# An attention mask added by VectorE in PSUM instead of by a matmul, with two steps of the tile loop moved forward, in a one-core audio tower kernel

## The reference

```python
h = tok_ref(x, W, b)                       # path signature of depth 4, projected to 128
h = h + attn_ref(layernorm(h), ...)        # 8 heads of 64, inner 512
h = h + ffn_ref(layernorm(h), ...)         # 8 experts, top 1, and a shared expert

# in attn_ref, for each sequence
dots = einsum('bhid,bhjd->bhij', q, k) * exp(temperature)
dots = where(eye(n), NEG_MAX, dots)        # a step does not see itself
attn = softmax(dots, axis=-1)
out = einsum('bhij,bhjd->bhid', attn, v)

# in tok_ref, the signature levels of the steps (k = 0..3)
acc = levels[k] + e[k]
for i in range(k): acc = acc + outer(levels[i], e[k - 1 - i])
```

## Time and profile before

| | |
|---|---|
| median of 3 runs | 694.17 us (692.53 to 695.29) |
| the profiled execution | 691.94 us |
| its span in the trace | 690.1 us |
| mean granted TensorE clock | 0.985 |
| first pass of the loop on TensorE | starts at 44.31 us |
| last pass (tile 31) | starts at 488.62 us |
| instructions | 13988 |

### The profile page before, as it was taken

How to read it: one execution, slowest core, us unless ns; L and a number is a source line. 1 busy time by engine, 2 the same in 40 slices (tenths; PEclk the granted TensorE clock), 3 DMA queues, 4 the chain that set the end, 5 groups by cost and what they waited for, 6 DMA issues and landing times.

```text
span 690.1 us, 13988 instructions
## 1 busy us (share of the span) xinstructions
PE 647.0 (94%) x3964; PEld 519.6 (75%) x3997; DVE 420.6 (61%) x1110; ACT 295.9 (43%) x702; POOL 322.1 (47%) x336
## 2 busy tenths in 40 slices
PE   5999999999999999999999999999789989999993
PEld 4677887788878888788877887776578957777772
DVE  7876666666666666766656666766436235455451
ACT  4234455434544445444454344443646334434340
POOL 2455454544545445444545444448534014545453
PEclk9999999999999999999999999999999999999997
DMA  8611344333634334343343431112354113232230
GB/s 308 270 35 31 78 104 95 90 93 76 146 83 99 84 80 118 77 107 76 93 105 83 100 77 39 34 36 73 99 195 138 43 46 44 37 44 39 39 40 5
DMA packets 70133, 59.70 MB, mean 87 GB/s; under 512 B 6752, under 2 KB 58848, under 8 KB 69728
## 3 DMA queue, kind: packets, MB, share of 16 engines
q1 hardware_dynamic: 63472, 55.21, 30.2%
q0 software_dynamic: 6640, 4.22, 4.4%
HBM read 16.78 MB, written 26.30 MB: 62 GB/s over the span
## 4 chain that ended last, share of the span: by engine, by line
PE 83%; DVE 6%; issue 4%; POOL 4%; DMA 1%; ACT 0%; SPq 0%; ACTq 0%; DVEq 0%; POOLq 0%
PE bank L1217 74%; PE bank L1539 3%; PE bank L1273 2%; PE bank L1426 2%; POOL sorted_rows L485 1%; POOL z L470 1%; PE bank L1522 1%; PE bank L1332 1%; PE bank L1323 0%; PE bank L1278 0%; POOL z L472 0%; PE bank L1277 0%; POOL out L558 0%; DVE utl L777 0%; DVE z L883 0%
## 5 line engine op out<-in xcount | busy, mean ns | idle before, releaser
L1217 PE MATMUL bank<-whigh,uth 128*128 128x512 f32 x512 | 169.1, 411 | 1.2 <-DVE lowt L777 1.2
L1217 PEld LDWEIGHTS bank<-whigh,uth 128*128 128x128 f32 x512 | 92.4, 190 | 28.0 <-issue 7.4
L558 POOL DMA_INDIRECT out<-prob,ids x39 | 60.9, 1561 | 94.0 <-ACT prob L740 92.5
L1217 PE MATMUL bank<-whigh,utl 128*128 128x512 f32 x256 | 101.6, 397 | 0.0
L479 POOL TENSOR_TENSOR rstd<-rstd,powers 128x1 f32<-128x1 f32 x64 | 35.3, 552 | 119.8 <-DVE rstd L870 64.5
L470 POOL TENSOR_TENSOR z<-z 128x512 f32<-128x512 f32 x32 | 42.3, 1323 | 90.9 <-DVE z L883 90.9
L1217 PE MATMUL bank<-xT,qkw 128*128 128x128 f32 x512 | 63.9, 279 | 0.0
L1190 DVE COPY xvp<-bank 128x512 f32<-128x512 f32 x39 | 27.0, 692 | 59.3 <-PE bank L1539 59.3
L1217 PEld LDWEIGHTS bank<-xT,qkw 128*128 128x128 f32 x512 | 61.3, 196 | 0.1
L1217 PEld LDWEIGHTS bank<-whigh,utl 128*128 128x128 f32 x256 | 48.4, 189 | 11.9
L883 DVE TENSOR_TENSOR z<-bank,v 128x512 f32<-128x512 f32 x64 | 44.1, 690 | 20.8 <-PE bank L1217 16.8
(11 more groups left out here) (227 smaller groups left out, 1439.2 us busy)
## 6 DMA issues: line engine op xcount, KB each, us to landing
sorted_rows<-blank SPq DMA_DIRECT2D x24, 709.5 KB, 5.7
xvp<-xvo SPq DMA_DIRECT2D x128, 128.0 KB
w<-w_t SPq DMA_DIRECT2D x1, 4096.0 KB, 12.3
xvo<-sorted_rows SPq DMA_DIRECT2D x39, 64.5 KB, 1.7
w<-w_high SPq DMA_DIRECT2D x4, 512.0 KB, 6.5
x_columns<-x2t SPq DMA_DIRECT2D x32, 64.0 KB
xg_in<-x_columns SPq DMA_DIRECT2D x8, 256.0 KB
levels<-w_t SPq DMA_DIRECT2D x1, 2048.0 KB, 7.5
```

What stands on the lines that cost most here:

```text
L558: nc.gpsimd.indirect_dma_start(out=out[:, :], out_offset=bass.IndirectOffsetOnAxis(ap=ids[:, j:j + 1], axis=0), in_=y[:, j % 2, :], in_off ...
L1217: return T.matmul(out_, lhsT, rhs, start=start, stop=stop)
```

## The change

The mask matmul and `ident_b` go. VectorE adds the mask to the scores in place, in PSUM, ahead of the row maximum, and waits for its own add with a new semaphore. On VectorE `level4` moves ahead of `finish` and of both `weigh` halves; on TensorE `features` moves ahead of `x2_columns`; on ScalarE `features_hi` moves ahead of `x2_transposed`.

```diff
@@ ScalarE, iteration
                 A.copy(pt[:].rearrange("k c s q -> k (c s q)"), B[6][:]).then_inc(pT_sb, 1)
+                if f:
+                    features_hi(i + 3)
                 if prev:
                     x2_transposed(i - 1, not older)
-                if f:
-                    features_hi(i + 3)
@@ VectorE, iteration
                 d.wait_ge(s_psum, i + 1)
+                V.tensor_tensor(B[4][:], B[4][:], mask[:], ALU.add).then_inc(masked, 1)
+                d.wait_ge(masked, i + 1)
                 sc = B[4][:].rearrange("p (c k) -> p c k", k=LEN)
...
                     finish = second_norm(i - 1, not older)
+                if f:
+                    level4(i + 3)
+                if prev:
+                    finish()
                 if u:
                     weigh(i + 2, 0)
-                if prev:
-                    finish()
-                if f:
-                    level4(i + 3)
-                if u:
                     weigh(i + 2, 1)
                 if f:
                     features_lo(i + 3)
@@ VectorE, ahead of the loop
-            V.tensor_copy(ident_b[:], ident).then_inc(consts_cast, 1)
             V.tensor_copy(mask[:], maskf).then_inc(consts_cast, 1)
@@ TensorE, iteration
-                T.matmul(B[4][:], ident_b[:], mask[:], start=True, stop=False)
                 for s in range(2):
                     last = mm(B[4][col(s, LEN), :], xT[:, col(s, LEN)],
-                              xqk[:, s, :, :].rearrange("p h k -> p (h k)"), False, True)
+                              xqk[:, s, :, :].rearrange("p h k -> p (h k)"))
...
                 if u:
                     project(i + 2, 9, 10)
+                if f:
+                    features(i + 3)
                 if prev:
                     x2_columns(i - 1)
...
-                if f:
-                    features(i + 3)
```

More of the change, by code:

```diff
@@ L145, in build @@
         before_r = sb("before_r", [P, P], F32R)
-        ident_b = sb("ident_b", [P, P], BF16)
         mask = sb("mask", [P, C3], BF16)
@@ L301, in build @@
         g_psum, g_sb, vo_psum, vo_sb = sem("xqk_psum"), sem("xqk_sb"), sem("xvo_psum"), sem("xvo_sb")
+        masked = sem("scores_masked")
         s_psum, soft, shifted, exp_done = sem("scores_psum"), sem("row_max"), sem("shifted"), sem("exp_done")
@@ L1068, in _ @@
                 remainder(vow[:, 1, cols], B[5 - n][:], vow[:, 0, cols], ww_lo)
-            d.wait_ge(consts_cast, 3)
+            d.wait_ge(consts_cast, 2)
             weigh(0, 0, True)
@@ L1482, in _ @@
             features(2)
-            pe.wait_ge(consts_cast, 2)
             pe.wait_ge(small, SMALL_STEPS)
```

## The result

The changed kernel takes 686.89 us (median of 4 runs, 686.38 to 688.08), the kernel before 693.35 beside it (4 runs, 691.65 to 695.29). The ratio is 0.991, with a 95% interval of 0.9892 to 0.9928, so it is faster by 6.5 us. 688.4 had been predicted. The profiled execution of the changed kernel is the longest of its four, 688.08, with a span of 685.9 us; the spans of the others are 684.5 to 684.9.

A forecast was written before the change was run, and what follows sets the result against it. TensorE, busy for 94% of the span, was taken to bound the loop, with GpSimd deciding late. Terms of -6.2, -0.3 and +0.7 sum to -5.8 us, from 694.17 to 688.4; range just below 685.9 to 691.8, plus the runs' spread.

The forecast's parts named there:

- The mask matmul: On TensorE ahead of the scores: removing it saves 0.22 us a tile, 6.2 us over tiles 0 to 27.
- the hole: Gap of 0.31 us ahead of the scores on TensorE: 0.22 for the mask matmul, 0.09 staying for the width change.
- The first rival: Ahead of the scores, all 0.31 us a tile goes: 2.5 us more saved, 685.9 us; chance 0.12.
- The add: On VectorE ahead of the row maximum: 0.69 us, at most 1.38, a step of 0.72, hidden in middle tiles.
- the slower rival: Writing PSUM doubles VectorE's add to 1.38 us, `xn` comes late, 697.5 us; sign decided at a 1.30 step; chance 0.05.
- The cover of `u`: At a pass's end `u` is ready 0.27 us ahead of its transposes, just enough; each 0.1 lost costs 2.8 us.
- The moves' worth: Reordering level 4 and the features' transposes makes `features` due 0.11 us earlier, gaining 0.33 us in the routing passes.
- Routing passes: Passes of tiles 26 to 28: 0.77 us gained, 0.44 from the mask and 0.33 from the moves.
- The sign to look for: TensorE's three waits for VectorE's copy of the logits should sum to 3.9 us, from 4.2.
- Late tiles: Savings of tiles 28 to 30 are lost to GpSimd's scatters; in tile 31 the add is exposed, costing 0.72 us.
- The rival of the clock: The longer wait in tile 31 lowers TensorE's clock: 1.5 us given back, 689.9 us; chance 0.08.
- The cast: Ahead of the loop, the mask's cast stands still beside GpSimd in `ident_b`'s place, some 2.8 us: 0 saved.

The follow-up runs named there:

- e2: Kernel before with only the three moves of level 4, the features' transposes and ScalarE's copies, mask matmul kept: 692.94 us, ratio 0.999.
- e4: Changed kernel with the mask matmul put back as well, matmul and add each bringing half of the mask: 693.74 us, ratio 1.0003.
- e1: Changed kernel with the add kept and all three moves taken back: 689.89 us, ratio 0.9949 to the kernel before.
- e11: Changed kernel with TensorE's and ScalarE's moves kept, but level 4 back in its old place on VectorE: 689.74 us, ratio 0.9955.
- e10: Changed kernel with level 4 moved forward on VectorE, but TensorE's and ScalarE's lists in the order of before: 692.41 us, ratio 0.9993.
- e5: Changed kernel with the mask by matmul in tile 31 and by the add elsewhere: 686.12 us, ratio 0.9905 to the kernel before.
- e7: Changed kernel with GpSimd's scatters of tiles 29 to 31 all behind its last root: 683.96 us, ratio 0.9846 to the kernel before.
- e3: Changed kernel with the add done twice, each with half of the mask's value: 691.43 us, ratio 0.9974 to the kernel before.
- e8: Changed kernel with the mask cast on ScalarE and the token bias sum behind VectorE's first two weigh steps: 687.88 us, ratio 0.9914.
- e12: Kernel of the add without the moves, TensorE's loop over tiles 2 to 25 unrolled by two: 689.39 us, ratio 0.9943 to the kernel before.
- c2: Changed kernel with the scatters of passes 29 to 31 behind the last root and the mask by matmul in tiles 30 and 31: 682.08 us, ratio 0.9834.

## Why the prediction was right, and where it was not

**The mask matmul: right.** 0.22 a tile had been priced, and 5.76 in 26 passes are 0.22 each. Of that 0.21 is the matmul's place (0.53 to 0.32), and 0.01 the moves', which gain 0.32 in the 26 passes by themselves (e2). The 0.09 that was left in the hole for the change of width is there: the second `z,sq` starts 0.11 behind the first, its place ends at 216.98 and the scores start at 217.08, 0.10 later. The page "TensorEngine Tiling (Array Packing)" of the Trainium skill, section Key Properties, says that a change of the tiling mode drains TensorE; the trace agrees, in that 0.10 are left between the two, though no run shows that TensorE is drained there. The first rival, that the whole hole goes, falls with it.

**The add: right.** 32 rows of 0.69 to 0.70, nothing lost in the loop (e4), and the bound of 1.38 wasn't reached. But the slower rival was priced too dear. I took 0.27 as the distance that a transpose needs, since the first pass shows it. With two adds a step is 1.45 and `xn` stands 0.08 ahead, and the pass loses 0.06, not 0.30 or more. The sign changes between a step of 1.45 (ratio 0.9974) and one of 2.20 (1.0271), not at 1.30. 0.27 was enough but not needed in the middle of a pass.

**The cover of `u`: right in its number, for a reason that I had not seen whole.** `u` ends 0.27 ahead, as worked out, and nothing is lost. The price of losing this cover, 2.8 us for each 0.1, isn't what the runs show. With a lead of 0.19 (e1) a pass loses 0.14, more than the whole shortfall; with one of 0.05 it loses 0.13 (e11, `u`) or 0.20 (e10, `x2n`). In e1 none of it stands at the transposes of `u`; it stands behind them, at the loop's branch. In e10 and e11 0.05 to 0.06 stand right behind the late transpose (in e10 0.04 ahead of it too) and the rest at the branch. It is the lead and not the order of the transposes: the kernel before has e1's order, with a lead of 0.38 for `u` (227.74 to 228.12), and its next first group takes 1.95. I had taken the 0.27 from tile 0, which is outside the hardware loop and has no branch behind it. That it held inside as well could not be seen from there.

**The moves' worth.** The prediction priced the moves at almost nothing (0.3 for routing) and the add at 6.2. The sum was right, but the parts aren't additive: e1 and e2 give 3.3 and 0.2. The moves are what lets the add's saving through: without them the pass end gives back 0.14 of 0.23. The prediction had worked out the leads for the change as a whole, so its sum holds, but it didn't say that the moves are needed.

**Routing passes: 1.03 against 0.77.** The moves' part was priced too high: alone they gain 0.19 in these passes (e2) and not 0.33, and the add alone gains 0.66 (e1). The third of them is the pass of tile 28, whose 0.22 I had counted as lost at once; TensorE's starts show it, and it is lost after them. The sign to look for was wrong. The waits for the logits sum to 3.1 and not 3.9, because the idle time before also held the mask matmul that has no record: 4.2 - 3 x 0.33 = 3.2. With the add alone (e1) they sum to 3.3, with the moves alone (e2) to 4.0.

**Late tiles: right.** From the loop's start to the sums of pass 28 on GpSimd 6.51 are gained, 6.49 by the prediction's terms. `z,sq` of tile 30 still waits for GpSimd. Up to the start of tile 31 TensorE has gained 6.92. Of the 0.43 above 6.49, GpSimd's list between the sums gives 0.36 (461.31 to 479.08 before, 455.52 to 472.93 after), and 0.34 of this is one scatter that took 1.30 before and 0.96 after. The prediction named only the sum as tile 30's wait. TensorE also waits there for the probabilities, 1.20 before and 1.24 after, and for `x2n`, 2.42 and 2.47. The add costs nothing in this tile because VectorE's `xn`, in the middle of the softmax, stands idle until GpSimd's root has ended, 1.06 before (root to 483.29, `xn` from 483.32) and 0.43 after (477.12, 477.16). Tile 31's wait for the probabilities grew from 0.50 to 1.46, and 0.86 is lost where 0.72 was predicted; e5 (20.84 us for this piece) shows that it is the add's. e7 shows that the scatters were the bound of tile 30.

**The rival of the clock: open, with more on its side than I had given it.** In the profiled execution the 1.2 GHz level lasted longer, and 1.14 us went there. From 480 to 520 the mean granted clock is 0.91 before and 0.87 after. It is 0.87 also in the seven other kernels that do the add in tile 31, have the scatters in their old place and reach tile 31 at this time (e1, e3, e4, e8, e10, e11, e12), and 0.91 or 0.92 in the three without that add (e2, e5, c2). But it is 0.91 also in e7, which has the add and a wait of 1.45. So it isn't shown that the longer wait causes it. Each of these is one execution, and for the executions without a trace it is not known where the level fell.

**The cast: right.** The mask's cast shows 2.75 where the earlier trace rows has 0.41, because it stands where `ident_b` stood, beside GpSimd's 2.84. Where `ident_b` is cast again (e4, e5, c2), that cast takes 2.54 or 2.55 and the mask's 0.41.

**The miss of 1.5 us** against the median has two parts that can be named: the trace gains 6.06 and not 5.8 (0.3), and the median of the kernel before was 694.17 in the three runs that I carried the sum to and 693.35 in the four beside the changed one (0.8). The rest, 0.4, is within the spread of four runs.

**What stays open.** Why a short lead costs more at a loop's branch than in the middle of a pass. e12 shows that the branch takes part, and not how. Nor is it shown what the lead has to be counted to. From `u`'s end to the weight load of its transposes it is 0.05 in the changed kernel (225.64 to 225.69), which loses nothing, and 0.08 in e1 (227.69 to 227.77), which loses 0.14; only counted to the transposes themselves (0.27 and 0.19) does the lead tell the one from the other. A lead between 0.19 and 0.27 was not tried.

## What to carry to other kernels

When a step is taken off the bounding engine, look for each result that another engine delivers to it, and count the lead that is left, at the end of a loop's pass above all: here 0.27 us was enough there and 0.19 lost 0.14 of the 0.23 us that a pass could gain, with no idle time in TensorE's rows ahead of the instruction that was late. Test a change of several parts as a whole and by halves, since parts worth nothing alone can be what lets another part through. And look at the first and last tiles apart: what is hidden in the loop is on the path there, and the old way can be kept for those tiles alone. Before a gain there is put down to the edit, lay the granted clock of the same stretch beside it.

## What the runs showed of the hardware

- A result that comes late at the end of a loop's pass costs TensorE time that the trace shows behind the matmul that needed it: up to 0.08 between the last matmul ahead of the branch and the first behind it, and 0.07 in the group of 16 short ones behind it (2.02 instead of 1.95). Without a branch between (e12) both are gone.
- Where a transpose's operand ended only 0.05 or 0.08 ahead of it, the step behind the transpose was 0.03 (e3) to 0.06 (e10) longer.
- An in-place add of 128x512 in PSUM takes VectorE 0.69 to 0.70 us, like one that writes SBUF.
- Scaling `xn` on VectorE (line 904) took 0.51 before and 0.34 after the change, though nothing in it changed; it starts at another moment of GpSimd's work now. Before, it ran from 221.63 to 222.14, inside a GpSimd instruction from 220.99 to 222.06; after, it starts at 220.49, when that instruction has ended (220.18). With the moves alone (e2) it runs inside it and takes 0.51.
- The switch from matmuls on 128 columns of the array to matmuls on 64 left 0.10 us between them.
